# One-hot comparisons of the front read their values from 16-bit pairs stored twice, and seven comparisons of an edge chunk become one

## The chip, the cores and the metric

The kernel runs on one core of a Trainium2 chip. The metric is the device time of one execution in microseconds (us). Before the change three runs gave 1142.17, 1131.55 and 1142.92 us; the median is 1142.17 us.

## The reference

The input is a graph with N = 50,000 nodes of 128 features (`x`) and E = 25,000 edges with 16 features each. Edges are sorted by their target `dst`; `src` is random.

```python
def _edge_conv(x, src, dst, edge_attr, W, b, denom):
    msg = jnp.concatenate([x[src], edge_attr], axis=1) @ W + b
    s = jax.ops.segment_sum(msg, dst, num_segments=x.shape[0])
    return s / denom[:, None]
...
counts = jax.ops.segment_sum(jnp.ones((src.shape[0],), x.dtype), dst, num_segments=x.shape[0])
denom = jnp.maximum(counts, 1.0)
h = _edge_conv(x, src, dst, edge_attr, W0, b0, denom)
outputs = [h]
for W, b in ((W1, b1), (W2, b2), (W3, b3)):
    cat = jnp.concatenate(outputs, axis=1)
    z = _edge_conv(cat, src, dst, edge_attr, W, b, denom)
    outputs.append(z)
...
x = _layernorm(x + outputs[-1], axis=-1)
```

So four edge convolutions run one after the other, and a layer norm of `x` plus the last of them over all 50,000 rows is the output.

## The kernel before

The kernel folds the four layers' weights together, sums messages per target node ("segment"), and then follows the graph for three more hops over short lists of the nodes that matter. The change touches only the first third, the front, and one loop behind it.

**Data layout.** Edges lie as 196 columns of 128 (T = 196), one edge per partition. A unit or chunk is HALF = 7 columns, so there are UNITS = 28 of them. To sum or to look things up by a value, the kernel builds one-hot matrices on the Vector engine (DVE): it compares a row of counting numbers (`iotah`, 0 to 255 in f16) with each edge's value, and TensorE (PE) multiplies with the matrix of zeros and ones.

**The front, in three stages.** Every engine runs its own program; semaphores tie them together.

- *Word stage* (`word_ones`, lines 1051 to 1060; on PE `word_sums`, L1847). For each of the 28 chunks DVE makes three tiles: `LA` compares 128 counting numbers with `lod` (L1055, 7 x 128 elements), `OHW` compares 49 with `hid` (L1059, 7 x 49), and `OHW` is multiplied by `value` (L1060). `lod` is f16, `hid` and `value` are f32 (names of the buffers `shi` and `nlo`). PE sums them into a table of words. LA and OHW have two buffers each, and DVE may be two chunks ahead (it waits on `tab_mm`).
- *Look-up stage* (`one_hot_src`, `pick`, `gather_words`, lines 1113 to 1136; on PE `look_up`, L1866). DVE makes `OS` from rows that a DMA has spread over all partitions (L1118, loaded by SP's `load_lows`, L477), then `WORD_HOT` (L1122, 49 wide, against `his`, f32 in buffer `nhi`), the product with what PE looked up (L1131) and its sum (L1136). A serial part of short instructions on DVE follows (lines 1170 to 1215).
- *Edge stage* (the loop of lines 1456 to 1466: `edge_ones`, `list_build`, `edge_add`, `list_add`; on PE `edge_chunk`, L1836 and L1840, and `list_chunk`, L1880). Per chunk DVE makes `SA` with seven instructions, each comparing 256 numbers with one column of `rela` (L1233), `SA2` (L1254, 7 x 128, against `list_lo`, f16), two small tiles (L1256, L1258), and adds PE's sums of the chunk before to `EC` and `AC` (L1243 to L1245, L1267). Before two of them it loads a row's place into registers (L1238, L1263). Every fourth chunk it also splits edge features (L1146 to L1149).

**What runs beside it.** In all three stages the 28 units of `x` run through as well: GpSimd (POOL) gathers seven columns of 128 rows of `x` by indirect DMA (L656), ScalarE makes their one-hots, PE sums them (`x_unit`, L1819 and L1827), and ScalarE adds the sums up (L799). PE's program fixes how these interleave:

```python
for u in range(UNITS):
    x_unit(u)
    if u < LOOK_UNIT:
        for c in range(u * 5, min(u * 5 + 5, UNITS)):
            word_sums(c)
```

With LOOK_UNIT = 6 and EDGE_UNIT = 13, units 0 to 5 carry five word chunks each, units 6 to 12 four look-up chunks each, and units 13 on two edge chunks each. POOL may gather two units ahead of PE's sums. SP's queue issues the clearing and copying of `x_and_z_of_nodes` (L485, L490) between the loads of rows and edge features.

**Behind the front** come the products of all segments on PE (L1915, L1916), with the making of the lists beside them. One loop there, `needed_build` (L1419), compares with `list_lo` in the same way as L1254. Three rounds over the lists and the layer norm end the program; the change doesn't touch them.

## Time and profile before

| what | value |
|---|---|
| median of three runs | 1142.17 us (1131.55 to 1142.92) |
| the profiled execution: its span, first to last instruction | 1122.8 us |
| what lies around the span, if that execution took the median time | 19.4 us |
| DVE busy | 739.8 us, 66% |
| POOL busy | 742.0 us, 66% |
| PE busy | 513.6 us, 46% |
| ScalarE busy | 476.3 us, 42% |
| word stage, look-up stage, serial part, edge stage (from the span's start) | 36 to 112.6, 112.6 to 188, 188 to 207.7, 207.7 to 378 us |

No engine is busy all the time, so the total shares decide nothing. What a faster instruction is worth has to be read in its own stage, from what the engines wait for there.

### The profile page before, as it was taken

How to read it: one execution, taken by the hardware profiler on the slowest of the kernel's cores; microseconds unless marked ns; L12 is line 12 of the kernel's file. 1: busy time of each engine (PE TensorE's matmuls, PEld its weight loads, DVE VectorE, ACT ScalarE, POOL GpSimd, SP SyncE). 2: the span in 40 equal slices, each digit the busy share in tenths (PEclk: the TensorE clock that was granted, in tenths of full speed). 3: DMA queues.
4: the chain of work that ended last, by engine and by line, in shares of the span. 5: the costliest groups of instructions: out<-in, count | busy, mean ns of one | idle time of the engine just before them, and what ended most of it. 6: DMA issues, size and time to landing. Idle time of an engine off the chain costs nothing.

```text
span 1122.8 us, 14207 instructions
## 1 busy us (share of the span) xinstructions
PE 513.6 (46%) x3128; PEld 379.0 (34%) x3128; DVE 739.8 (66%) x2530; ACT 476.3 (42%) x1099; POOL 742.0 (66%) x669
## 2 busy tenths in 40 slices
PE   1544653578776578878775360054005664000000
PEld 0433552455555345545343250043005553000000
DVE  6788677878766776454765558566767976679100
ACT  8543343334433155556554213571547541156200
POOL 6788666377675066666676647774877773777775
PEclk9666666666566589899898665566556766555555
DMA  6895457599999046455555846995899983464111
GB/s 189 229 299 154 114 133 197 149 261 324 316 304 340 6 153 218 165 202 178 180 173 175 268 138 148 301 318 179 221 291 327 336 294 118 118 222 143 50 52 34
DMA packets 224618, 224.99 MB, mean 200 GB/s; under 512 B 19218, under 2 KB 206475, under 8 KB 224495
## 3 DMA queue, kind: packets, MB, share of 16 engines
q1 hardware_dynamic: 193551, 153.22, 44.1%
q0 software_dynamic: 26624, 44.81, 15.0%
q10 hardware_dynamic: 4320, 25.56, 5.7%
q8 instruction: 47, 0.77, 0.3%
q14 instruction: 76, 0.62, 0.2%
HBM read 117.11 MB, written 132.74 MB: 223 GB/s over the span
## 4 chain that ended last, share of the span: by engine, by line
DVE 29%; PE 24%; POOL 16%; issue 15%; DMA 7%; another core or an unknown queue 4%; ACT 2%; DVEq 2%; SPq 1%; POOLq 0%; ACTq 0%
POOL out_rows L724 5%; POOL G L685 5%; PE segp L1827 4%; POOL part_rows L698 3%; PE hp L1916 3%; DVE AC L1586 3%; DVE area L1233 3%; PE segp L1916 2%; DMA area<-x_and_z_of_nodes 2%; POOL EC L717 2%; PE lp L1840 2%; PE segp L2056 2%; PE hp L2056 2%; DVE area L1254 2%
## 5 line engine op out<-in xcount | busy, mean ns | idle before, releaser
L656 POOL DMA_INDIRECT G<-x_in,srci x196 | 229.1, 1169 | 114.3 <-issue 62.2
L668 POOL DMA_INDIRECT x_and_z_of_nodes<-area,sum_rows x144 | 146.0, 1014 | 102.3 <-ACT area L826 65.2
L854 ACT ACTIVATE area<-area,AC 128x128 f32<-128x128 f32 x299 | 117.5, 480 | 44.4 <-DVE AC L1608 37.4
L799 ACT ACTIVATE UT<-segp,UT 128x1 f32 x56 | 14.6, 261 | 207.4 <-PE segp L1827 150.6
L685 POOL DMA_INDIRECT G<-part_rows,s0r x70 | 80.1, 1144 | 27.3 <-issue 18.3
L1827 PEld LDWEIGHTS segp<-SX,G 128*128 128x128 f32 x392 | 92.9, 319 | 14.0 <-issue 5.4
L1827 PE MATMUL segp<-SX,G 128*128 128x128 f32 x392 | 94.2, 409 | 5.7 <-ACT SX L788 3.2
L2050 PE MATMUL segp<-ZERO 128*128 128x390 f16 (+1 forms) x34 | 15.3, 449 | 163.0 <-DVE EC L1628 152.5
L717 POOL DMA_INDIRECT EC<-x_and_z_of_nodes,idx x60 | 64.7, 1079 | 33.4 <-issue 17.9
L826 ACT ACTIVATE area<-hp,zero,inv 128x512 f32<-128x512 f32 x72 | 53.9, 781 | 44.4 <-PE hp L1916 15.3
L826 ACT ACTIVATE area<-segp,zero,inv 128x512 f32<-128x512 f32 x72 | 54.6, 780 | 41.2 <-PE hp L1916 20.8
L724 POOL DMA_INDIRECT out_rows<-UT,idx x60 | 59.2, 986 | 18.3 <-issue 18.3
L1916 PE MATMUL hp<-LATE,UT 128*128 128x384 f32 x144 | 64.9, 535 | 0.0
L847 ACT ACTIVATE AC<-AC,eps 128x13 f32<-128x13 f32 x30 | 9.2, 306 | 131.0 <-DVE AC L1594 95.8
L1840 PE MATMUL lp<-area 128*128 128x52 bf16 x392 | 54.7, 213 | 18.8 <-issue 8.9
L2056 PE MATMUL segp<-G,EC 128*128 128x130 f32 (+1 forms) x272 | 55.2, 368 | 17.1 <-DMA G<-part_rows,s0r 7.8
L1916 PE MATMUL segp<-LATE,UT 128*128 128x384 f32 x144 | 61.2, 508 | 0.0
L1586 DVE BATCH_NORM_STATS2 AC<-area 128x6 f32<-128x128 f32 x299 | 60.1, 278 | 0.8
L784 ACT ACTIVATE SX<-iota,rel 128x128 f32<-128x128 f32 x196 | 60.4, 395 | 0.0
L2050 PEld LDWEIGHTS segp<-ZERO 128*128 128x128 f16 x34 | 4.0, 116 | 166.6 <-DVE EC L1628 159.8
L2056 PEld LDWEIGHTS segp<-G,EC 128*128 128x128 f32 x272 | 52.2, 276 | 22.8 <-DMA G<-part_rows,s0r 9.5
L2056 PE MATMUL hp<-G,EC 128*128 128x130 f32 (+1 forms) x232 | 49.4, 380 | 16.6 <-DMA G<-part_rows,s0r 8.9
(468 smaller groups left out, 1599.5 us busy)
## 6 DMA issues: line engine op xcount, KB each, us to landing
part_rows<-area SPq DMA_DIRECT2D x36, 768.0 KB
area<-x_and_z_of_nodes SPq DMA_DIRECT2D x30, 832.0 KB
x_and_z_of_nodes<-ZERO SPq DMA_DIRECT2D x24, 1024.0 KB
x_and_z_of_nodes<-x_in SPq DMA_DIRECT2D x24, 1024.0 KB
area<-x_in SPq DMA_DIRECT2D x23, 832.0 KB
out_rows<-area ACTq DMA_DIRECT2D x23, 832.0 KB
part_rows<-ZERO SPq DMA_DIRECT2D x14, 768.0 KB
area<-src_low_rows SPq DMA_DIRECT2D x28, 224.0 KB
```

Of the source, the lines that this page charges most:

```text
L656: g.indirect_dma_start(G[:, slot, 0:D], None, x, bass.IndirectOffsetOnAxis(ap=srci[:, c:c + 1].bitcast(u32), axis=0), bounds_check=last_no ...
L668: g.indirect_dma_start(XZ2, bass.IndirectOffsetOnAxis(ap=sum_rows[:, c:c + 1], axis=0), HS3[:, b, j, 3 * D:4 * D], None, bounds_check=last ...
L685: g.indirect_dma_start(G[:, n % GS, 0:D], None, TB3, bass.IndirectOffsetOnAxis(ap=take[k][:, n:n + 1], axis=0), bounds_check=last_part, oo ...
L717: g.indirect_dma_start(LZ[:, 2 * r + w, :], None, XZ[0:N, :], bass.IndirectOffsetOnAxis(ap=node_u[:, b:b + 1], axis=0), bounds_check=last_ ...
L724: g.indirect_dma_start(out, bass.IndirectOffsetOnAxis(ap=node_u[:, b:b + 1], axis=0), own_row(b, W1), None, bounds_check=last_node, oob_is ...
L826: a.activation(HS3[:, b, j, :], PBANK[j][:, :], ACT.Identity, bias=zero1[:, 0:1], scale=inv[:, g * CG + j:g * CG + j + 1]).then_inc(s["p_a ...
L854: last = a.activation(XLS[b][:, k], XLS[b][:, k], ACT.Identity, bias=shift[:, b, r:r + 1], scale=rs[:, b, r:r + 1])
L1586: last = v.bn_stats(stat[cols, b, r, :], src_[cols, r * D:(r + 1) * D])
L1827: t.matmul(SG[q][:, bass.ds(w, P)], G[:, slot, 0:D], S[:, slot, :], start=False, stop=j == hi - 1).then_inc(s["summed"], 1)
L1840: last = t.matmul(LP[b][:, bass.ds(k + w * ES64, EP)], SA[:, b * HALF + j, w * P:(w + 1) * P], EB[:, q % 2, (c % EQ) * HALF + j, 0:EP], st ...
L1916: t.matmul(PBANK[j][:, 0:3 * D], UT[:, (g * CG + j) * P:(g * CG + j + 1) * P], M[:, :], start=False, stop=True).then_inc(s["p_mm"], 1)
L2056: last = t.matmul(bank[:, bass.ds(at_, width)], OH[:, g % OHG, j, w * P:(w + 1) * P], G[:, slot, 0:width], start=False, stop=j == 1 and w ...
```

## The change

All wide comparisons named above get a form in which every operand is 16 bits wide and its innermost step is one. Each compared value is stored twice, side by side, in f16: `low_pairs` (an own buffer in place of `lod` and `list_lo`), and `value_pairs`, `hid_pairs`, `his_pairs`, `rela_pairs`, which lie in the f32 buffers `nlo`, `shi`, `nhi` and again `nlo`. A comparison then walks over the counting numbers two at a time, and over a pair again and again, instead of over one value with step 0. The width of 49 becomes 50. The seven instructions of `edge_ones` become one over 7 x 256 elements.

```diff
+        low_pairs = sb("low_pairs", [P, CT, 2], f16)
+        in_pairs = lambda a: a[:, :].bitcast(f16).rearrange("p (t w) -> p t w", w=2)
+        value_pairs, hid_pairs, his_pairs, rela_pairs = in_pairs(nlo), in_pairs(shi), in_pairs(nhi), in_pairs(nlo)
...
-            link(v.tensor_tensor(value[:, et], bits_src[:, et], flag[:, et], ALU.mult))
+            twice = lambda a: a[:, et].unsqueeze(2).to_broadcast([P, T, 2])
+            link(v.tensor_tensor(value_pairs[:, et, :], twice(bits_src), twice(flag), ALU.mult))
-            link(v.tensor_copy(lod[:, et], ints[:, et]))
+            link(v.tensor_copy(low_pairs[:, et, :], twice(ints)))
-            link(v.tensor_copy(hid[:, et], ints[:, et]))
+            link(v.tensor_copy(hid_pairs[:, et, :], twice(ints)))
...
+            def in_twos(tiles):
+                return tiles.rearrange("p j (w t) -> p j w t", t=2)
+            def spread_pairs(pairs, c, width):
+                return pairs[:, c * HALF:(c + 1) * HALF, :].unsqueeze(2).to_broadcast([P, HALF, width // 2, 2])
+            def ones_by_pairs(tiles, pairs, c, width):
+                places = iotah[:, 0:width].rearrange("p (w t) -> p w t", t=2).unsqueeze(1).to_broadcast([P, HALF, width // 2, 2])
+                return v.tensor_tensor(in_twos(tiles), places, spread_pairs(pairs, c, width), ALU.is_equal)
...
-                v.tensor_tensor(LA[:, b, :, :], iotah[:, 0:P].unsqueeze(1).to_broadcast([P, HALF, P]),
-                                lod[:, c * HALF:(c + 1) * HALF].unsqueeze(2).to_broadcast([P, HALF, P]), ALU.is_equal)
-                link(v.tensor_tensor(OHW[:, b, :, 0:WORDS], iotah[:, 0:WORDS].unsqueeze(1).to_broadcast([P, HALF, WORDS]), spread_out(hid), ALU.is_equal))
-                v.tensor_tensor(OHW[:, b, :, 0:WORDS], OHW[:, b, :, 0:WORDS], spread_out(value), ALU.mult).then_inc(s["oh_built"], 1)
+                ones_by_pairs(LA[:, b, :, :], low_pairs, c, P)
+                link(ones_by_pairs(OHW[:, b, :, :], hid_pairs, c, WORDS + 1))
+                words = in_twos(OHW[:, b, :, :])
+                v.tensor_tensor(words, words, spread_pairs(value_pairs, c, WORDS + 1), ALU.mult).then_inc(s["oh_built"], 1)
...
-            link(v.tensor_copy(his[:, et], ints[:, et]))
+            link(v.tensor_copy(his_pairs[:, et, :], twice(ints)))
+            link(v.tensor_copy(rela_pairs[:, et, :], twice(rela)))
...
-                v.tensor_tensor(WORD_HOT[:, b, :, :], iotah[:, 0:WORDS].unsqueeze(1).to_broadcast([P, HALF, WORDS]),
-                                his[:, k].unsqueeze(2).to_broadcast([P, HALF, WORDS]), ALU.is_equal).then_inc(s["hot_words"], 1)
+                ones_by_pairs(OHW[:, b, :, :], his_pairs, c, WORDS + 1).then_inc(s["hot_words"], 1)
...
-            link(v.tensor_scalar(list_lo[:, et], wlo[:, et], -1.0, None, ALU.add))
+            link(v.tensor_scalar(low_pairs[:, et, :], twice(wlo), -1.0, None, ALU.add))
...
-                for j in range(HALF):
-                    last = v.tensor_scalar(SA[:, (c % 2) * HALF + j, :], iotah[:, :], rela[:, c * HALF + j:c * HALF + j + 1], None, ALU.is_equal)
-                last.then_inc(s["e_built"], 1)
+                ones_by_pairs(SA[:, (c % 2) * HALF:(c % 2 + 1) * HALF, :], rela_pairs, c, 2 * P).then_inc(s["e_built"], 1)
...
-                v.tensor_tensor(SA2[:, b, :, :], iotah[:, 0:P].unsqueeze(1).to_broadcast([P, HALF, P]),
-                                list_lo[:, chunk].unsqueeze(2).to_broadcast([P, HALF, P]), ALU.is_equal)
+                ones_by_pairs(SA2[:, b, :, :], low_pairs, c, P)
```

`needed_build` changes as `list_build` does (`CLO` in place of `SA2`), and its `list_lo` is made in pairs too. `pick` goes on reading 49 of the 50 columns.

No instruction changes its place among the others. On DVE, at the start of the edge stage, before the change (the buffers `SA` and `SA2` lie in `area`):

```order
L1223 CAST area<-nh 128x28
L1224 CAST area<-nl 128x28
L1225 COPY area<-flag 128x28
L1233 TENSOR_SCALAR area<-iotah,rela 128x256 x7
L1254 TENSOR_TENSOR area<-iotah,list_lo 128x896
L1256 TENSOR_TENSOR area<-iota,nodes 128x56
L1258 TENSOR_TENSOR area<-LATE,area 128x336
```

And with the change (`nlo` holds `rela_pairs`; L1064 is the comparison in `ones_by_pairs`):

```order
L1235 CAST area<-nh 128x28
L1236 CAST area<-nl 128x28
L1237 COPY area<-flag 128x28
L1064 TENSOR_TENSOR area<-iotah,nlo 128x1792
L1064 TENSOR_TENSOR area<-iotah,low_pairs 128x896
L1265 TENSOR_TENSOR area<-iota,nodes 128x56
L1267 TENSOR_TENSOR area<-LATE,area 128x336
```

The seven instructions of 256 elements are one of 1792; everything else stands where it stood. The one added instruction of the program is the copy to `rela_pairs` ahead of the look-up stage.

## Rows read from the trace of the kernel before

**Rows 1.** Stages: busy us of PE, PEld, DVE, ACT, POOL; PEclk, DMA share, GB/s.
```profile
36.00:112.60 76.60, 34.17 (x294) 29.98 (x294) 59.22 (x104) 33.61 (x101) 63.61 (x49) 0.59 0.84 239
112.60:188.00 75.40, 43.91 (x504) 38.79 (x504) 55.24 (x131) 34.48 (x105) 50.10 (x47) 0.66 0.50 130
207.70:378.00 170.30, 127.59 (x838) 93.76 (x839) 130.53 (x436) 61.59 (x189) 103.11 (x88) 0.61 0.86 261
```

**Rows 2.** Chain of waits, shares by line: word stage, look-up stage, edge stage.
```profile
by line: PE segp L1827 23.7%; DVE area L1055 20.4%; issue 15.4%; DVE area L1060 11.8%; DVE area L1059 9.8%; PE segp L1819 7.9%; PE tp L1847 7.2%; ACT SX L788 1.0%; DVE area L1107 0.5%; DVE area L1096 0.4%; PE tp L1871 0.3%; DVE area L1095 0
...
by line: issue 26.8%; PE segp L1827 18.1%; PE lp L1866 13.1%; DMA area<-src_low_rows 9.2%; DVE idx L1136 7.2%; PE segp L1819 6.0%; DVE area L1122 5.4%; DVE area L1131 4.8%; DVE area L1118 4.5%; SPq L477 1.7%; DVE area L1147 0.9%; DVE area L
...
by line: DVE area L1233 17.3%; issue 15.0%; PE lp L1840 12.1%; DVE area L1254 10.0%; PE segp L1827 8.9%; DVEq L1263 4.4%; DVEq L1238 3.5%; DVE EC L1243 3.2%; PE segp L1819 3.0%; DVE EC L1244 2.9%; DVE EC L1245 2.9%; PE lp L1836 2.7%; DVE AC
```

**Rows 3.** Groups on DVE by shape, 0 to 560 us: busy us, mean ns | idle before.
```profile
L1233 DVE TENSOR_SCALAR area<-iotah,rela 128x256 bf16<-128x256 f16 x196 | 41.4, 295 | 3.8 <-DVE AC L1267 0.6 <-issue 0.3 <-PE lp L1840 0.3
...
L1254 DVE TENSOR_TENSOR area<-iotah,list_lo 128x896 bf16<-128x896 f16 x28 | 30.3, 1081 | 0.0
...
L1258 DVE TENSOR_TENSOR area<-LATE,area 128x336 bf16<-128x336 bf16 x28 | 14.3, 509 | 1.0
...
L1118 DVE TENSOR_SCALAR area<-area,iotap 128x896 f16<-128x896 f16 x28 | 13.2, 470 | 2.3 <-DMA area<-src_low_rows 1.0 <-issue 0.7 <-DVE area L1149 0.2
...
L1146 DVE CAST area<-area 128x448 bf16<-128x448 f32 x7 | 2.7, 390 | 0.3 <-DVE area L1225 0.2
```

**Rows 4.** Timeline of DVE in the word stage, one chunk and the next: start, us.
```profile
59.49 1.08 DVE L1055 TENSOR_TENSOR area<-iotah,lod 128x896 f16<-128x896 f16 x1
60.49 0.51 DVE L1059 TENSOR_TENSOR area<-iotah,shi 128x343 f16<-128x343 f16 x1
61.04 0.52 DVE L1060 TENSOR_TENSOR area<-area,nlo 128x343 f16<-128x343 f16 x1
61.47 1.08 DVE L1055 TENSOR_TENSOR area<-iotah,lod 128x896 f16<-128x896 f16 x1
```

**Rows 5.** Timeline of PE in the word stage, from one x unit to the next.
```profile
63.55 0.58 PE L1819 MATMUL segp<-ZERO 128*128 128x512 f16 x1 [1.46 <-issue]
...
67.34 0.79 PE L1847 MATMUL tp<-area 128*128 128x49 f16 x14
70.01 0.47 PE L1847 MATMUL tp<-area 128*128 128x49 f16 x7 [1.88 <-DVE area L1060]
...
75.92 0.58 PE L1819 MATMUL segp<-ZERO 128*128 128x512 f16 x1 [1.49 <-issue]
```

**Rows 6.** Timeline of POOL in the word stage: a gather beside idle DVE, one beside L1055.
```profile
54.11 1.00 POOL L656 DMA_INDIRECT G<-x_in,srci  x1 [0.30 <-issue]
...
59.76 1.68 POOL L656 DMA_INDIRECT G<-x_in,srci  x1 [0.30 <-issue]
```

**Rows 7.** Groups on POOL by shape: word stage, then edge stage.
```profile
L656 POOL DMA_INDIRECT G<-x_in,srci x41 | 54.4, 1326 | 12.4 <-issue 12.4
...
L656 POOL DMA_INDIRECT G<-x_in,srci x88 | 103.1, 1172 | 55.3 <-issue 25.4 <-PE segp L1827 23.6 <-remote 6.3
```

**Rows 8.** Chain of waits in the look-up stage, one piece: start, us, what.
```profile
139.97 3.53 DMA area<-src_low_rows
```

**Rows 9.** Timeline of DVE in the edge stage, from one chunk to the next.
```profile
310.98 1.46 DVE L1233 TENSOR_SCALAR area<-iotah,rela 128x256 bf16<-128x256 f16 x7
312.35 1.08 DVE L1254 TENSOR_TENSOR area<-iotah,list_lo 128x896 bf16<-128x896 f16 x1
...
315.66 1.47 DVE L1233 TENSOR_SCALAR area<-iotah,rela 128x256 bf16<-128x256 f16 x7
```

**Rows 10.** Waits in the edge stage: us in total, times, longest us.
```profile
PE lp L1836 <- DVE area L1233: 9.1, 7, 3.1
```

**Rows 11.** Timeline and group on DVE: the old cast to `list_lo`; `needed_build`.
```profile
205.59 0.26 DVE L1215 TENSOR_SCALAR list_lo<-wlo 128x196 f16<-128x196 f32 x1
...
L1419 DVE TENSOR_TENSOR area<-iotah,list_lo 128x896 bf16<-128x896 f16 x10 | 11.0, 1098 | 0.0
```

More of the change, by code:

```diff
@@ L213, in gnn_kernel @@
         xoff = wlo[:, :].bitcast(i32)
-        value, hid, his, src_low = nlo, shi, nhi, idx
+        src_low = idx
+        in_pairs = lambda a: a[:, :].bitcast(f16).rearrange("p (t w) -> p t w", w=2)
+        value_pairs, hid_pairs, his_pairs, rela_pairs = in_pairs(nlo), in_pairs(shi), in_pairs(nhi), in_pairs(nlo)
         AREA = 8584
@@ L237, in gnn_kernel @@
         list_hi, list_block = nodes, inv[:, :].bitcast(i32)
-        list_lo = sb("list_lo", [P, T], f16)
         list_hi2, list_block2 = nodes, nodec[:, :].bitcast(i32)
@@ L1412, in needed_places @@
                 link(v.tensor_tensor(wlo[:, et], wlo[:, et], need[:, et], ALU.mult))
-                link(v.tensor_scalar(list_lo[:, et], wlo[:, et], -1.0, None, ALU.add))
+                link(v.tensor_scalar(low_pairs[:, et, :], twice(wlo), -1.0, None, ALU.add))
             def needed_build(c):
@@ L1418, in needed_build @@
                     e.wait_ge(s["c2_mm"], c - 1)
-                v.tensor_tensor(CLO[:, b, :, :], iotah[:, 0:P].unsqueeze(1).to_broadcast([P, HALF, P]),
-                                list_lo[:, places_of(c)].unsqueeze(2).to_broadcast([P, HALF, P]), ALU.is_equal)
+                ones_by_pairs(CLO[:, b, :, :], low_pairs, c, P)
                 one_hots(CHOT[:, b, :, :], list_hi2, c, HALF + 1).then_inc(s["c2_hot"], 1)
```

4 lines of the change are left out of this document (removed).

## The prediction, made before the changed kernel had run

> **What bounds the kernel now.** I read the table by stage first, since the change lies in the front alone. In the word stage [rows 1] DVE is busy 59.2 of 76.6 us and POOL 63.6, PE only 34.2. In the edge stage DVE is busy 130.5 of 170.3 us, PE 127.6, POOL 103.1. No engine fills a stage, so the engines must be waiting in turn, and the chain of waits is the second view [rows 2]. In the word stage it runs through the three instructions that change, L1055, L1059 and L1060: 42% of 76.6 us. In the look-up stage only 5.4% lie on L1122. In the edge stage L1233 and L1254 hold 17.3% and 10.0% of 170.3 us, with PE's L1840 (12.1%) close behind.
>
> The timelines show how a turn goes. DVE needs 61.47 - 59.49 = 1.98 us per word chunk [rows 4]. PE takes 12.37 us from one x unit to the next [rows 5]: the unit itself, two chunks that lay ready (67.34), then three more that it waits for (from 67.8 to 74.4), then 1.5 us before the next unit. DVE is only two chunks ahead, so three chunks in five are on the path. In the edge stage a chunk takes DVE 4.68 us when it never waits [rows 9], but 170.3 / 28 = 6.1 us on average.
>
> **What one instruction will take.** Two 16-bit comparisons with a step of 0, of 896 and 336 elements, take 1081 and 509 ns [rows 3]. That is 572 / 560 = 1.02 ns per element plus 166 ns. The trace has no two-input operation of the new form (16 bits, innermost step one everywhere), so its rate is bounded. The slow end is no gain, 1.02 ns. The fast end is L1118, 896 elements of one input in 470 ns: (470 - 166) / 896 = 0.34 ns. Between them lies L1146, 448 elements in 390 ns: 0.50 ns. I take 0.50, since two inputs must be fetched where L1118 fetches one, and keep both ends.
>
> The Trainium skill, "Vector Engine (DVE) Microarchitecture Reference", section 5.1, says that a two-input operation runs two elements per tick if all operands have 2 bytes, an innermost step of one and more than one element innermost, and that one element read again and again runs at one per tick. By that rule the old form is slow and the new one twice as fast. No row here shows the new half; the 1.02 ns of the old form agree.
>
> **The change, part by part.**
>
> - *Word stage.* L1055 goes from 1.08 us to 166 + 448 = 0.61 (-0.47). L1059 and L1060 each go from 0.51 to 166 + 175 = 0.34 (-0.17, with 350 instead of 343 elements). A chunk's pitch falls from 1.98 to 1.17 us. By the chain [rows 2] L1055 holds 15.6 us of the path, 15 pieces at about 1.0 us, and L1059 and L1060 7.5 and 9.0 us, 14 and 16 pieces: 15 x 0.47 + 30 x 0.17 = 12.2 us. The turn of PE [rows 5] gives the same: 3 chunks x 0.81 = 2.4 us for each of five units, and 0.8 for the last. Is something late next? POOL's gathers for a unit now end only some 7 us before PE takes it up, and POOL never waits for PE in this stage (its 12.4 us of idle are all issue, [rows 7]). A gather takes 1.00 us while DVE rests and 1.68 beside L1055 [rows 6], on average 1.33, so with 0.3 of issue a unit of seven costs POOL 11.4 us against a new turn of PE of 12.4 - 2.4 = 10.0. If DVE's holds become half as long, a gather averages perhaps 1.2 (an estimate between the 1.00 and the 1.33 of these rows), a unit 10.5 us. That nearly keeps up: I take **-12**, and -5 if the gathers stay at 1.33.
> - *Look-up stage.* L1122 loses 0.17 us; 5.4% of 75.4 us are 8 pieces on the path, so 1.4 us. But the load of the next rows takes 3.53 us [rows 8] and only two are ahead, so a faster chunk waits for it. I take **-1**.
> - *Edge stage.* The seven L1233 end 1.46 us after they start, and L1254 starts 1.37 after [rows 9]. One instruction of 1792 elements takes 166 + 896 = 1.06 us: -0.40. L1254 goes from 1.08 to 0.61: -0.47. The chain holds 29.5 us of L1233, 20 chunks, and 17.0 us of L1254, 17 chunks: 20 x 0.40 + 17 x 0.47 = 16 us at most. PE is close behind, though, with 127.6 us of work of its own; its explicit waits for L1233 add up to 9.1 us [rows 10]. The gain lies between about 5 and 16; I take **-10**.
> - *Behind the front.* L1419 runs ten times at 1.10 us [rows 11]; 10 x 0.48 = 4.8 us, beside PE's products. I take **-1**.
> - *Added.* The five stores in pairs and the one copy more handle 392 elements instead of 196. The cast to `list_lo` takes 0.26 us [rows 11], so each costs at most that much more. Those ahead of the word and look-up stages lie where DVE would be ahead of PE, the one at L1215 is on a serial path. Without the cover all would cost 1.5 us; I take **+0.5**.
>
> The sum is -12 - 1 - 10 - 1 + 0.5 = -23.5 us. The profiled execution's span is 1122.8 us; the new one would be 1099. The time around the span (19.4 us if that execution was the median one) doesn't change, so against the median of 1142.17 I predict **1118 us**. Runs of before lie 1% apart, so 1% is about what a measurement can tell from no change.
>
> Transfers must not be late either. The copies of `x_and_z_of_nodes` fill DMA in the edge stage (share 0.86 on average, [rows 1]). They aren't on its chain of waits, and POOL's scatters that need them come after 378 us, so I count nothing.
>
> **The rivals.**
>
> *The next in line takes over (chance 0.25).* POOL stays at 1.33 us per gather and PE's own work sets the edge stage. Then -5 in the word stage, -6 in the edge stage, nothing elsewhere: about 1131 us. For it: POOL is the busiest engine of the word stage, and PE and DVE are nearly equal in the edge stage. Against it: POOL's slow gathers stand beside DVE's long instructions, which get shorter.
>
> *The pairs run no faster (0.07), the case on the slower side.* If two inputs stay at 1.02 ns in this form too, L1055 and L1254 gain nothing, and one instruction of 1792 elements takes 166 + 1828 = 1.99 us in place of 1.46, since the seven of 256 ran at 1.46 / 1792 = 0.8 ns and lost that rate with their scalar. On 20 chunks of the path that is +11 us, with the casts about +12: 1154 us. Where does it turn? At a rate of 0.72 ns, (1460 - 166) / 1792, the new instruction takes as long as the old seven, and the other pieces on the path still gain; with them the sum reaches zero at about 0.88 ns per element. For it: no row shows the form. Against it: 16-bit operands of step one with one input do run fast.
>
> *More than the sum (0.08).* If the comparisons come near L1118's rate, or shorter holds bring the gathers to 1.0 us, each stage gives more: the instruction of 1792 would take 0.78 us (0.28 more on 20 chunks, 5.6 us), L1055 and L1254 0.14 more on 32 pieces (4.6 us). -34 us, 1108.
>
> A longer hold of POOL is the other side of the edge stage: one DVE instruction of 1.06 us where seven short ones left gaps. The trace agrees that a gather gets longer beside L1055 (1.68 against 1.00 us). In the edge stage gathers average 1.17 us and POOL waits for PE 23.6 us [rows 7], so 88 gathers could each grow by 0.2 us and stay hidden; hence no term.
>
> **How the numbers follow.** The forecast has a chance of 0.60 (its own range 1112 to 1125), the rivals 0.25, 0.07 and 0.08. Faster by over 1% means below 1130.7: all of the forecast and of the larger gain, over half of the first rival: 0.83. Within 1%: the rest of that rival, 0.10. Slower: 0.07. The range of 8 in 10 takes in the first rival and half of the larger gain: 1105 to 1134.
>
> **What would show it.** In the profile after, the comparison of 896 elements takes about 0.61 us, that of 1792 about 1.06, those of 350 about 0.34; the word stage lasts 64 to 65 us and the edge stage 160; gathers of the word stage fall from 1.33 us on average towards 1.2; PE's waits for the edge comparisons shrink; behind the front all stages last as long as before. The prediction is wrong if the 896 take more than 0.8 us, or if POOL's gathers or PE's issue fill the time that DVE frees.

## The result, and the profile after the change

The change gained nothing. In 20 runs each, one beside the other, the kernel before took 1137.62 us (median) and the changed one 1142.36 us; the ratio is 1.006, with a 95% interval of 1.0035 to 1.0085. Here and below the ratios leave out runs in the slower state, over 1.5% above the fastest of their kernel (one of `after_few` took 2280.08 us), so they aren't exactly the quotients of the medians. I had predicted 1118 us and a range that ended at 1134.

The profiled execution of the changed kernel has a span of 1148.2 us, that of before 1122.8 us. Such a pair exaggerates the difference, so I compare parts. Let the **front** end where DVE adds the last list chunk to `AC` (L1267 before, L1276 after). It ended at 375.9 us before and at 385.7 us after. What lies behind took 746.8 us before. In the 16 further profiles below that leave the transfers in place it was 742 to 750 us, with the change and without it, and only here 762.5 us. So some 15 us of the difference belong to this one execution, and the change itself acts in the front alone. That is what I read below. A stage's time in one profile is uncertain too: the four kernels below that have the word stage, the gathers and the transfers as they were (before, edge_only, edge_seven, old_word) end it at 110.0 to 112.6 us.

The instructions did what was forecast. Groups on DVE of the changed kernel, 0 to 600 us (busy us, mean ns | idle before), against [rows 3]:

```profile
L1064 DVE TENSOR_TENSOR area<-iotah,nlo 128x1792 bf16<-128x1792 f16 x28 | 30.6, 1094 | 3.7
...
L1064 DVE TENSOR_TENSOR area<-iotah,low_pairs 128x896 bf16<-128x896 f16 x38 | 23.6, 621 | 0.0
...
L1064 DVE TENSOR_TENSOR area<-iotah,low_pairs 128x896 f16<-128x896 f16 x28 | 18.4, 656 | 41.0 <-PE tp L1855 22.9 <-remote 18.1
...
L1073 DVE TENSOR_TENSOR area<-area,nlo 128x350 f16<-128x350 f16 x28 | 10.9, 388 | 1.0
...
L1064 DVE TENSOR_TENSOR area<-iotah,shi 128x350 f16<-128x350 f16 x28 | 9.3, 334 | 0.0
```

1094, 621 and 334 ns stand where 1.06, 0.61 and 0.34 us were forecast. (1094 - 621) / 896 is 0.53 ns per element; I had taken 0.50, and the old form ran at 1.02. By the Trainium skill's rule that the prediction quoted ("Vector Engine (DVE) Microarchitecture Reference", section 5.1) the new form is twice as fast, and the trace agrees. But look at the idle time in the third line: DVE stood still for 41.0 us ahead of the word comparison. The stages, as in [rows 1] (busy us of PE, PEld, DVE, ACT, POOL; PEclk, DMA share, GB/s):

```profile
36.00:118.90 82.90, 33.65 (x293) 29.49 (x294) 37.85 (x103) 33.85 (x101) 53.05 (x48) 0.58 0.79 222
118.90:201.20 82.30, 46.65 (x504) 40.85 (x504) 50.60 (x133) 34.62 (x105) 50.92 (x49) 0.65 0.46 125
220.60:387.80 167.20, 127.11 (x840) 93.65 (x840) 107.63 (x267) 61.97 (x190) 97.20 (x89) 0.59 0.87 265
```

In the word stage DVE's work fell from 59.2 to 37.9 us and POOL's from 63.6 to 53.1, yet the stage grew from 76.6 to 82.9 us. The look-up stage with the serial part grew from 94.7 to 101.3 us (both from the start of unit 6 to the first payload copy of the edge stage), and the edge stage shrank from 170.3 to 167.2. In the word stage no engine's work grew by more than 0.3 us. The chain of waits of the word stage, by line, names the new holder, against [rows 2]:

```profile
by line: another core or an unknown queue 23.2%; PE segp L1835 18.3%; issue 16.8%; DVE area L1064 16.3%; DVE area L1073 7.8%; PE tp L1855 6.1%; PE segp L1827 5.4%; ACT SX L789 0.9%; DVE area L1109 0.3%; DVE area L1098 0.3%; DVE area L1090 0
```

"Another core or an unknown queue" (in the timelines: "remote") isn't among the lines of this chain before. There is only one core, so the label means that the profile found no row that ended just before the wait did. The timelines of three engines at one place show what it stands for. DVE of the changed kernel in the word stage (start, us):

```profile
48.23 0.35 DVE L1073 TENSOR_TENSOR area<-area,nlo 128x350 f16<-128x350 f16 x1
58.35 0.63 DVE L1064 TENSOR_TENSOR area<-iotah,low_pairs 128x896 f16<-128x896 f16 x1 [9.77 <-remote]
...
62.16 0.63 DVE L1064 TENSOR_TENSOR area<-iotah,low_pairs 128x896 f16<-128x896 f16 x1 [2.56 <-remote]
...
65.87 0.63 DVE L1064 TENSOR_TENSOR area<-iotah,low_pairs 128x896 f16<-128x896 f16 x1 [2.46 <-remote]
```

PE at the same place:

```profile
50.84 1.48 PE L1835 MATMUL segp<-SX,G 128*128 128x128 f32 x6
52.12 0.64 PE L1855 MATMUL tp<-area 128*128 128x49 f16 x14
59.66 0.47 PE L1855 MATMUL tp<-area 128*128 128x49 f16 x7 [6.91 <-DVE area L1073]
```

And POOL, the last gathers of a series of 14:

```profile
61.46 1.00 POOL L657 DMA_INDIRECT G<-x_in,srci  x1 [0.30 <-issue]
62.76 1.15 POOL L657 DMA_INDIRECT G<-x_in,srci  x1 [0.30 <-issue]
73.94 1.15 POOL L657 DMA_INDIRECT G<-x_in,srci  x1 [10.03 <-PE segp L1835]
```

PE's 14 products end at 52.76 us (as modelled), and two increments of `tab_mm`, the semaphore that DVE waits for, go with them. DVE needs the first of them and starts at 58.35, more than 5 us later; the second releases it at 62.16. The trace records the increments themselves at 58.33 and 62.14 us. The next product, over at 60.13, is told at 65.85. POOL's gathers end at 63.9, and from 65.93 us on nothing is behind (the product that ends at 67.66 is told at 67.67). So a word from PE travels for microseconds while POOL issues gathers.

I counted this over the whole front. An increment of PE is **late** here if the trace records it more than 0.25 us after the end of the last instruction of PE that makes it and has ended by then. (Where several increments are held up together this counts from the last product, so it gives too small delays rather than too large ones.) In the profile of before, of those made during a series of gathers or within 1 us behind one, 133 of 228 are late, by up to 7.7 us; of the 55 made at other times, none. In the other direction the words are prompt: no increment of DVE in the front of before is recorded more than 0.03 us behind its row, and 34 of PE's 38 starts that DVE releases follow within 0.06 us. The other four, all products of the look-up, start 0.84 to 3.02 us behind DVE's row.

In the edge stage PE's own issue stutters as well. PE of the changed kernel while a series of gathers runs (to 252.87 us), and behind it:

```profile
248.39 0.22 PE L1848 MATMUL lp<-area 128*128 128x52 bf16 x1 [1.87 <-issue]
249.13 0.22 PE L1848 MATMUL lp<-area 128*128 128x52 bf16 x1 [0.52 <-issue]
250.75 0.22 PE L1848 MATMUL lp<-area 128*128 128x52 bf16 x1 [1.40 <-issue]
251.40 0.22 PE L1848 MATMUL lp<-area 128*128 128x52 bf16 x1 [0.43 <-issue]
253.48 0.20 PE L1848 MATMUL lp<-area 128*128 128x52 bf16 x1 [1.85 <-issue]
254.18 0.20 PE L1848 MATMUL lp<-area 128*128 128x52 bf16 x1 [0.49 <-issue]
255.13 0.84 PE L1848 MATMUL lp<-area 128*128 128x52 bf16 x4 [0.74 <-issue]
255.87 0.44 PE L1888 MATMUL hp<-area 128*128 128x48 bf16 x7
```

Single products with up to 1.9 us of "issue" between them, and then seven in 0.44 us. DVE's add of that chunk (L1253) waited 12.27 us for them.

The Trainium skill, "Perfetto Trace Analysis", section "Summary: the profiler window per engine type", says that TensorE's row ends at an estimate, and that the time until a semaphore has arrived is hidden from the row. The trace agrees: no row above covers the time between the product that ends at 52.76 and the waiter that starts at 58.35. The page doesn't say how long that time may be.

### The profile page after: what moved, and what is told of

The parts are those of the page before. It is cut to its first block, busy times and chain, and to the rows that moved or that the text cites. A ratio compares the mean times of both kernels' runs of the same rounds, so it can differ in the third digit from the quotient of the medians.

```text
span 1148.2 us, 14017 instructions
## 1 busy us (share of the span) xinstructions
PE 507.1 (44%) x3105; PEld 374.1 (33%) x3128; DVE 683.6 (60%) x2363; ACT 478.0 (42%) x1099; POOL 727.5 (63%) x669
## 4 chain that ended last, share of the span: by engine, by line
DVE 28%; PE 24%; issue 15%; POOL 12%; another core or an unknown queue 9%; DMA 7%; ACT 2%; DVEq 1%; SPq 0%; POOLq 0%; ACTq 0%
POOL out_rows L725 5%; PE segp L1835 4%; DVE AC L1594 4%; POOL part_rows L699 4%; DVE area L1064 3%; PE hp L1924 3%; PE segp L1924 3%; PE lp L1848 3%; DMA area<-x_and_z_of_nodes 3%; DVE area L1609 2%; POOL EC L718 2%; DVE UT L1650 1%; PE segp L1827 1%; PE hp L2064 1%
## 5 line engine op out<-in xcount | busy, mean ns | idle before, releaser
L657 POOL DMA_INDIRECT G<-x_in,srci x196 | 210.2, 1073 | 144.9 <-PE segp L1835 66.4
L1848 PE MATMUL lp<-area 128*128 128x52 bf16 x392 | 54.7, 214 | 27.4 <-issue 17.7
L1064 DVE TENSOR_TENSOR area<-iotah,low_pairs 128x896 bf16<-128x896 f16 (+1 forms) x66 | 42.0, 636 | 41.0 <-PE tp L1855 22.9
L848 ACT ACTIVATE AC<-AC,eps 128x13 f32<-128x13 f32 x30 | 9.2, 307 | 137.1 <-DVE AC L1602 108.1
L2064 PE MATMUL segp<-G,EC 128*128 128x130 f32 (+1 forms) x272 | 52.7, 356 | 29.3 <-DMA G<-part_rows,previ 13.1
L699 POOL DMA_INDIRECT part_rows<-UT,nlo x24 | 44.8, 1865 | 20.7 <-DVE UT L1705 13.7
```

The source lines that it names most:

```text
L657: g.indirect_dma_start(G[:, slot, 0:D], None, x, bass.IndirectOffsetOnAxis(ap=srci[:, c:c + 1].bitcast(u32), axis=0), bounds_check=last_no ...
L699: g.indirect_dma_start(TB3, bass.IndirectOffsetOnAxis(ap=l2_at[k - 1][:, b:b + 1], axis=0), own_row(b, w), None, bounds_check=last_part, o ...
L1848: last = t.matmul(LP[b][:, bass.ds(k + w * ES64, EP)], SA[:, b * HALF + j, w * P:(w + 1) * P], EB[:, q % 2, (c % EQ) * HALF + j, 0:EP], st ...
L2064: last = t.matmul(bank[:, bass.ds(at_, width)], OH[:, g % OHG, j, w * P:(w + 1) * P], G[:, slot, 0:width], start=False, stop=j == 1 and w ...
```

## The experiments

All ratios are to the kernel before, run beside each kernel on the same chip, with 95% intervals; it took 1122 to 1127 us there, 1137.62 beside the changed kernel. The table collects what the sections use. "Unit 6" is the start of the seventh x unit on PE, the end of the word stage; "late" is the share of PE's increments between 36 us and the end of the front that are late, and the last column sums the delays of all of them. Each row but the ratio is from one profile.

| kernel | ratio | unit 6 | front ends | late | delays, us |
|---|---|---|---|---|---|
| before | | 112.6 | 375.9 | 48% | 259 |
| changed | 1.006 (1.0035 to 1.0085) | 118.9 | 385.7 | 52% | 346 |
| before_late | 1.119 (1.113 to 1.126) | 106.6 | 382.0 | 37% | 164 |
| after_late | 1.119 (1.113 to 1.126) | 111.0 | 374.1 | 53% | 321 |
| word_only | 1.0046 (1.0006 to 1.0085) | 116.8 | 379.7 | 49% | 261 |
| edge_only | 0.9946 (0.9916 to 0.9977) | 110.0 | 369.9 | 54% | 312 |
| edge_seven | 1.0011 (0.9982 to 1.0040) | 111.0 | 382.0 | 48% | 281 |
| old_word | 1.0007 (0.9975 to 1.0039) | 112.4 | 373.7 | 47% | 283 |
| word_pad | 1.0035 (1.0005 to 1.0066) | 113.7 | 377.8 | 49% | 284 |
| word_ring | 1.0003 (0.9968 to 1.0037) | 109.9 | 378.5 | 54% | 399 |
| after_ring | 1.0037 (1.0004 to 1.0070) | 111.0 | 378.4 | 54% | 400 |
| before_few | 0.9751 (0.9706 to 0.9796) | 111.8 | 355.8 | 1% | 6 |
| after_few | 0.9486 (0.9443 to 0.9529) | 99.4 | 321.1 | 0% | 5 |
| before_pause | 1.0050 (1.0022 to 1.0078) | 112.7 | 387.4 | 25% | 118 |
| after_pause | 0.9963 (0.9921 to 1.0006) | 111.7 | 372.9 | 32% | 146 |
| after_pause_again | 0.9930 (0.9895 to 0.9964) | 110.7 | 369.2 | 32% | 146 |
| after_two | 0.9952 (0.9923 to 0.9980) | 109.1 | 366.4 | 22% | 48 |
| before_each | 0.9930 (0.9899 to 0.9961) | 111.0 | 371.5 | 26% | 83 |
| after_each | 0.9814 (0.9756 to 0.9872) | 108.1 | 356.6 | 45% | 188 |
| after_tick | 1.0089 (1.0053 to 1.0124) | 118.8 | 385.3 | 52% | 355 |

### Are the transfers the pace? before_late and after_late

```diff
-            clear_sums(range(0, Z_AT[0]))
...
             for q in range(2, NQ):
                 load_features(q)
-                copy_x(range((q - 2) * XPIECES // (NQ - 2), (q - 1) * XPIECES // (NQ - 2)))
+            clear_sums(range(0, XPIECES))
+            copy_x(range(0, XPIECES))
```

> The kernel before, with all 25 clearing and 25 copying transfers of x_and_z_of_nodes issued after the last load of edge features, so that none runs beside the front. Same work, other order. Theory A (transfers set the pace of the front): before them the front had DMA shares of 0.76 and 0.87 in word and edge stage; without them the x units come faster, and unit 27, which started at 374.8 us, starts before 355 us. Theory B (PE's hand-offs to DVE or the engines' own work set it): unit 27 starts within 5 us of 374.8. The whole is slower in either case, since some 50 MB that moved at 300 GB/s then stand by themselves: 1230 to 1310 us. The run serves as the partner of after_late.

> The changed kernel with the same transfers put behind the front. Theory A: what DVE saves now reaches the end of the front: unit 27 starts 12 to 22 us ahead of before_late's, and the whole takes 10 to 22 us less than before_late. Theory B (late hand-offs, or gathers of POOL, eat the gain without any help from the transfers): within 5 us of before_late, both at unit 27 and in the whole.

Measured: unit 27 started at 382.1 us in before_late, where theory A wanted less than 355 and B 370 to 380, and at 374.4 in after_late. The transfers aren't the pace of the front: A falls. But they aren't without effect, as B has it. The word stage ended 6.0 and 7.9 us sooner without them (106.6 and 111.0 us), and after_late's unit 27 came 7.7 us before before_late's, between what A (12 to 22) and B (less than 5) had asked. What before_late lost behind the word stage stays open. The two whole times are the same (1252.68 and 1253.65 us), but that tells little, since the moved transfers form the end of this stretch in both and can hide what the front gives. Late words from PE are as frequent in after_late (53%), with a DMA share of 0.15 to 0.33 from 46 to 90 us, as in the changed kernel with 0.97 to 1.07, so DMA traffic alone isn't what makes them late (in before_late 37% were, against 48% in before).

### Which stage loses? word_only, edge_only, edge_seven, old_word

Each undoes part of the change. word_only keeps only the word stage's pairs:

```diff
-                ones_by_pairs(OHW[:, b, :, :], his_pairs, c, WORDS + 1).then_inc(s["hot_words"], 1)
+                v.tensor_tensor(WORD_HOT[:, b, :, :], iotah[:, 0:WORDS].unsqueeze(1).to_broadcast([P, HALF, WORDS]),
+                                his[:, k].unsqueeze(2).to_broadcast([P, HALF, WORDS]), ALU.is_equal).then_inc(s["hot_words"], 1)
...
-                ones_by_pairs(SA[:, (c % 2) * HALF:(c % 2 + 1) * HALF, :], rela_pairs, c, 2 * P).then_inc(s["e_built"], 1)
+                for j in range(HALF):
+                    last = v.tensor_scalar(SA[:, (c % 2) * HALF + j, :], iotah[:, :], rela[:, c * HALF + j:c * HALF + j + 1], None, ALU.is_equal)
+                last.then_inc(s["e_built"], 1)
```

> Only the word stage in pairs; look-up, edge stage and the loop behind the front as before. The word comparison of 896 elements takes 0.62 us. By my prediction, had it held, 12 us less than before (1.1%). Theory A: the transfers fill the word stage up to 90 us and the edge stage from 183 us; the word stage gives little and the edge stage takes back what is left: within 4 us of before. Theory C (a faster word stage disturbs what comes later: DVE's operations collide with POOL's gathers or its waits for PE get longer): slower than before by 3 to 8 us, so that the whole loss of the change is here.

edge_only has both edge comparisons (and the loop behind the front) in pairs, the word and look-up stages as before:

> Only the edge stage (and the loop behind the front) in pairs, the word and look-up stages as before. My prediction gave 10 us less. Theory A (the copies of x_and_z_of_nodes fill DMA from 183 us on, share 0.87, and SP's loads of edge features stand in the same queue behind them): within 4 us of before. Theory D (one operation of 1.09 us holds up POOL's issue of gathers where seven short ones left gaps): slower by 3 to 8 us, gathers of the edge stage over 1.25 us on average instead of 1.17.

edge_seven is edge_only with the seven short comparisons put back:

> edge_only with the seven short comparisons kept, so that only the comparison of 896 elements in the edge stage (and the loop behind the front) is in pairs. edge_only was 6 us faster than before. If the two edits give what they save on the path, this one gives about half: -3 us. If one operation of 1792 elements is what helps: within 2 us of before. If the one long operation hurts and the shorter list comparison helps: 6 us or more faster than before.

old_word is the changed kernel with the old word stage:

> The changed kernel with the word stage as before (old form, old values) and the look-up stage, the edge stage and the loop behind the front in pairs. edge_only, which lacks the look-up stage's pairs, was 6 us faster than before. If the word stage alone is what costs: 4 to 9 us faster than before. If the look-up comparison costs too: within 2 us of before.

Measured: the word stage's pairs cost 0.46%, about 5 us (theory C's size). The profiles agree: with the pairs the word stage ended at 116.8 us (word_only) and 118.9 (changed), without them at 110.0 to 112.6. The edge stage's give 0.54%, 6 us, so theory D falls, and A's "within 4 us" too. The one wide operation makes the gain: without it (edge_seven) nothing is left, where I had expected 3 us. old_word, with the look-up's pairs besides, is at 1.0007 where 4 to 9 us less were expected if the word stage alone costs. So the look-up's comparison, 0.17 us shorter, seems to cost 0.6% against edge_only (the two intervals leave 0.0 to 1.2%, and the two kernels ran on different chips). In the profiles the stretch from unit 6 to the first payload copy lasts 99.6 us in old_word, 101.3 in the changed kernel and 100.7 in after_ring, against 94.6 to 95.9 in before, edge_only, word_only and word_pad, which keep the old look-up; but edge_seven and word_ring, which keep it too, have 99.1 and 99.6. So the word stage loses by a faster DVE, and the look-up stage probably does, by about 4 us; that isn't shown clear of the noise.

### The pace or the form? word_pad

```diff
+                link(v.tensor_tensor(LA[:, b, :, 0:88], iotah[:, 0:88].unsqueeze(1).to_broadcast([P, HALF, 88]),
+                                     low_pairs[:, c * HALF:(c + 1) * HALF, 0:1].to_broadcast([P, HALF, 88]), ALU.is_equal))
                 ones_by_pairs(LA[:, b, :, :], low_pairs, c, P)
```

> word_only with one superfluous comparison more per word chunk, in the old form over 7 x 88 elements (about 0.79 us by 166 ns + 1.02 ns per element), so that DVE's pitch per chunk is again about 1.96 us, with the pairs kept. Theory P (the pace: DVE two chunks ahead no longer covers a late word from PE; with DVE slow it does): unit 2 starts at 62 to 65 us again instead of 69, and the whole is within 2 us of before. Theory F (the form of the operations: 16-bit pairs disturb another engine whatever the pace): unit 2 still starts near 69 us, and the whole stays 4 us or more above before.

Measured: unit 2 started at 65.7 us, between the 63.5 of before and the 69.0 of word_only, and unit 6 at 113.7 instead of 116.8. A DVE slowed down with work of no use brought the stage three of its four lost us back, with the pairs in place. So in the word stage the pace matters more than the form, as far as one profile each can tell: 3.1 us is little more than the 2.6 by which equal word stages differ. The whole (1.0035 against 1.0046) doesn't decide it.

### More cover? word_ring and after_ring

```diff
-                b = c % 2
-                if c >= 2:
-                    e.wait_ge(s["tab_mm"], c - 1)
-                ones_by_pairs(LA[:, b, :, :], low_pairs, c, P)
+                if c >= 4:
+                    e.wait_ge(s["tab_mm"], c - 3)
+                ones_by_pairs(LAR[c % 4], low_pairs, c, P)
```

`LAR` and `OHR` take their third and fourth buffers from `SA` and `ECS`, which are free in this stage.

> word_only with four buffers for LA and OHW instead of two, so that DVE may be four chunks ahead of PE. Theory L (PE's increments reach DVE 2 to 6 us after PE's last product of the chunk, which two buffers can't bridge): with four, a late one is bridged; unit 2 starts before 62 us, the word stage is 6 to 12 us shorter than in word_only, the whole 4 to 12 us faster than before. Theory Q (PE itself is behind its modelled ends, its own rate bounds the stage): no gain, unit 2 again near 69 us and the whole 3 to 6 us above before.

> The changed kernel with the same four buffers in the word stage. Theory L: the edge stage's gain, which edge_only showed (-6 us), and the word stage's add up: 10 to 18 us faster than before. Theory Q: within 3 us of the changed kernel (+5 us).

Measured: unit 2 started at 51.8 us, 17 us ahead of word_only, as L said. Then it was given back: unit 3 at 69.7, unit 6 at 109.9. The whole is at 1.0003 against word_only's 1.0046, not the 4 to 12 us below before that L named; after_ring, at 1.0037, is where Q put it. DVE of word_ring where it was lost:

```profile
58.60 0.62 DVE L1071 TENSOR_TENSOR area<-iotah,low_pairs 128x896 f16<-128x896 f16 x1 [5.82 <-PE tp L1866]
...
64.57 0.62 DVE L1071 TENSOR_TENSOR area<-iotah,low_pairs 128x896 f16<-128x896 f16 x1 [4.72 <-PE tp L1866]
```

Seven increments of unit 2's sums, whose products end between 53.7 and 58.3 us, are recorded from 65.94 to 66.21 us, 0.045 us apart, although a sum takes 0.43 us: those products had long been done, and the words came in one burst. POOL's series ended at 64.0. Both theories were half right: buffers bridge a late word, but here the hold-up lasted to the end of POOL's series, and four buffers don't reach that far.

### Without the gathers: before_few and after_few

```diff
-                for j in range(HALF):
+                for j in range(HALF if u < 2 else 1):
...
-                            e.wait_ge(gat[u % 2 * 4 + j // 2], (32 if j < HALF - 1 else 16) * (u // 2 + 1))
+                            e.wait_ge(gat[u % 2 * 4 + j // 2], (32 if j < HALF - 1 else 16) + (16 * (u // 2) if j == 0 else 0))
```

> The kernel before with only one gather of x rows per unit from unit 2 on instead of seven; the other six columns use rows that were gathered for units 0 and 1, so the sums of x are not the reference's, while all the work of PE, DVE and ScalarE stays. Theory G (POOL's gathers hold up PE's increments: in the profile of before 133 of the 228 increments of PE that fall in or within 1 us behind a series of gathers are over 0.25 us late, and none of the 55 outside): without the series at most a tenth of PE's increments in the front are over 0.25 us late, and unit 27 starts 15 us or more ahead of 374.8 us. Rival R (PE's own work is behind its modelled ends): as many are late as before, up to 5 us, and unit 27 moves by less than 10 us.

> The changed kernel with the same gathers left out. Theory G: PE's increments come in time here too, and what DVE saves reaches the end of the front: unit 27 starts 15 to 30 us ahead of before_few's, and the whole takes 12 to 30 us less than before_few. Rival R, or a bound by PE's own work: less than 5 us between the two.

Both kernels leave out six of seven gathers from unit 2 on, and so sum rows of `x` that aren't the right ones.

Measured: late words fell from 48% and 52% to 1% and 0%, with PE's program untouched, and unit 27 of before_few started at 354.7 us, 20 earlier. Between the two kernels there are now 0.9751 - 0.9486 = 0.0265 of 1126.2 us, 30 us: the gain that I had predicted (23.5), and more (the medians, 1103.17 and 1070.46 us, lie 33 us apart). Unit 27 of after_few came 33 us before before_few's. Windows of before_few, word stage and edge stage:

```profile
36.00:111.80 75.80, 33.03 (x294) 28.99 (x294) 58.41 (x104) 34.45 (x102) 18.51 (x13) 0.62 0.77 212
190.00:356.00 166.00, 122.03 (x830) 90.83 (x831) 130.57 (x438) 63.48 (x193) 12.48 (x12) 0.64 0.81 243
```

And of after_few:

```profile
36.00:99.40 63.40, 32.66 (x294) 28.76 (x294) 37.26 (x103) 34.31 (x102) 15.32 (x13) 0.67 0.92 253
180.00:321.00 141.00, 112.21 (x824) 85.39 (x824) 105.58 (x266) 61.67 (x188) 13.82 (x12) 0.69 0.92 278
```

The word stage is 12.4 us shorter; the prediction said 12. The edge stage, from its first payload copy to the front's end, fell by 22.9 us (163.6 to 140.7), where I had said 10 and 16 at most. Two things can be behind the excess, and no run parts them. With PE in time, more of DVE's chunks may have been on the path than the chain of before showed. And in these windows the granted clock was 0.69 in after_few against 0.64, and PE was busy for 112.2 us instead of 122.0 with nearly the same products, so up to 10 us of PE's work may have gone with the clock. The word stage is free of this: there PE's work is 32.7 against 33.0 us. PE's turn at the place of [rows 5] is the one that I had drawn, two chunks at once and three at 1.17 us each:

```profile
52.19 0.79 PE L1855 MATMUL tp<-area 128*128 128x49 f16 x14
54.03 0.35 PE L1855 MATMUL tp<-area 128*128 128x49 f16 x7 [1.05 <-issue]
55.19 0.35 PE L1855 MATMUL tp<-area 128*128 128x49 f16 x7 [0.81 <-DVE area L1073]
56.36 0.35 PE L1855 MATMUL tp<-area 128*128 128x49 f16 x7 [0.81 <-DVE area L1073]
```

Theory G holds, R falls. This pair changes several things at once, though: POOL's work and the gathers' transfers leave the path too. The next runs keep all gathers.

### Gaps between the gathers: after_pause, before_pause, after_two

```diff
                     slot = c % BODY
+                    if j == 3:
+                        for _ in range(5):
+                            plink(g.memset(rest[:, :], 0.0))
```

`plink` makes POOL wait for each memset; `rest` is a tile of its own. before_pause has the same edit in the kernel before, and after_two asks for `j in (2, 5)`.

> The changed kernel with a pause in each series of gathers: five short POOL memsets of 128 x 128 f32, each waited for, ahead of the fourth gather of a unit (some 1 to 1.5 us per unit). Theory G: PE's increments that were held up come through in the pause, so the longest delay falls from 11 us to about half a series (5 us); the time moves by -10 to +15 us, since POOL's series gets longer by the pause, and is no test by itself. Rival R: the pause changes nothing in when they come.

> The same kernel as after_pause, in more rounds beside the three others: 0.996 of before, interval within 0.4% of it.

> The kernel before with the same pause (five short memsets ahead of the fourth gather of a unit). Theory G: in the word stage DVE's long operations already stretch and part the gathers, so that few increments of PE are late there, and PE's late ones are in the look-up and edge stages; the pause lengthens POOL's series by 1.5 us per unit and gives back less than with the fast DVE: within 4 us of before. Rival H (the pause helps whatever DVE does): 4 us or more faster than before, as much as it gave the changed kernel.

> The changed kernel with two pauses in each series, ahead of the third and the sixth gather (2 x 1.5 us per unit). Theory G: the delays get shorter still (sum under 146 us in the front), but POOL's series of 9.2 us becomes 12.3, longer than the 11.3 us that a unit takes, so POOL's own work bounds the edge stage: 0 to 12 us slower than with one pause.

Measured: giving POOL more to do made the changed kernel faster, from 1.006 of before to 0.9963 and 0.9930 in two sets. The sum of the delays fell from 346 to 146 us, the longest from 11.2 to 6.5. In before the same pause cost 0.5%, 6 us, a little more than the 4 that G allowed. That is the crossed result that G wanted and H excluded: the pause helps with the fast DVE and costs with the slow one, although it cut the delays there as well (259 to 118 us). Two pauses cut the delays to 48 us, and the time is the same as with one (0.9952), presumably since POOL's longer series takes back what the words give.

### Small gaps: after_each, before_each, after_tick

after_each puts one memset, waited for, ahead of each gather but the first of a unit. before_each does it in the kernel before. after_tick has no memset, only an increment of POOL's own semaphore and the wait for it:

```diff
+                    if j:
+                        plink.n += 1
+                        e.sem_inc(s["pool_chain"], 1)
+                        e.wait_ge(s["pool_chain"], plink.base + plink.n)
```

> The changed kernel with one short memset, waited for, ahead of each gather but the first of a unit (6 x 0.25 us per unit, as long in all as the one pause). Theory G with gaps of any length: increments come through at each gap, sum of delays below 146 us, time at or below that with one pause. If a gap must last about 1 us: the delays stay as in the changed kernel (over 250 us in all) and the time is 3 to 10 us above before.

> The kernel before with one short memset, waited for, ahead of each gather but the first of a unit, as in after_each (0.981 of before). Theory G (gaps let PE's increments through, and the changed kernel gains most because its fast DVE left the gathers closest together and waits for PE most): before_each lies between, 0 to 10 us faster than before, so that the change itself is worth 10 us or more between before_each and after_each. Rival S (the gaps are worth the same with or without the change, 20 to 25 us): 0.975 to 0.985 of before.

> The changed kernel with no memset but an increment of POOL's own semaphore and a wait for it ahead of each gather but the first. If what counts is that POOL's queue runs empty between two gathers, even for 0.1 us: as after_each, 0.977 to 0.987 of before. If it is the time that the memset adds to the gap (the next gather starts 0.49 us after the last instead of 0.30): little, 1.000 to 1.007, as the changed kernel.

POOL of after_each in the word stage:

```profile
50.94 0.22 POOL L660 MEMSET rest<- 128x128 f32 x1
51.43 1.00 POOL L661 DMA_INDIRECT G<-x_in,srci  x1 [0.27 <-POOL rest L660]
52.43 0.22 POOL L660 MEMSET rest<- 128x128 f32 x1
52.92 1.00 POOL L661 DMA_INDIRECT G<-x_in,srci  x1 [0.27 <-issue]
```

Measured: with a gather every 1.49 instead of every 1.30 us the changed kernel takes 0.9814 of before, 1106.33 against 1126.31 us; it is the best version found. Without the change the same gaps give 0.9930. So with gaps the change is worth about 1.2%, some 13 us, and without them it costs 0.6%. after_tick, at 1.0089, gained nothing, and its profile tells why it couldn't:

```profile
48.32 0.99 POOL L661 DMA_INDIRECT G<-x_in,srci  x1 [0.30 <-issue]
49.62 0.99 POOL L661 DMA_INDIRECT G<-x_in,srci  x1 [0.30 <-issue]
```

Its gathers stand 1.30 us apart, as without the tick: the increment and the wait disappear in the 0.30 us that were there, so this run made no gap. It shows that one more wait in POOL's program does nothing, but not whether a gap without an operation in it would help. One figure missed: the delays of after_each sum to 188 us, not below 146, and 45% are late. So the count of late words doesn't order the times; I take it that what counts is whether the word that somebody waits for is late, but no count here shows that. The windows of after_each (word and edge stage):

```profile
36.00:108.10 72.10, 33.45 (x294) 29.29 (x294) 38.99 (x103) 33.61 (x101) 58.73 (x84) 0.62 0.89 254
201.10:358.70 157.60, 124.51 (x838) 92.56 (x839) 107.57 (x268) 61.54 (x189) 115.71 (x165) 0.64 0.93 283
```

72.1 and 157.6 us, where the prediction had 64 to 65 and 160.

## Why the prediction was wrong

**Durations of the new form: right.** 0.62 to 0.66, 1.09 and 0.33 us, for 0.61, 1.06 and 0.34. Only the product (L1073, 388 ns) stayed above its 0.34. Two of the inputs were loose: the 0.50 ns per element came from a cast of one input (L1146), and L1258, which I called a comparison, is a product. "The pairs run no faster", my one rival on the slower side, named the wrong cause.

**The word stage, -12 us: this step failed.** It was worked out from the chain and from PE's turn as rows show it, and both take it that DVE may go on when PE's row ends; the time for PE's word to arrive was put at nothing. In before that was nearly so: of the 65 increments of PE in the word stage 8 were late, and DVE's two chunks of lead at 1.98 us each covered them. With chunks of 1.17 us the lead is used up sooner, DVE waits, and what it waits for is under POOL's series: 11 of 61 increments were late in the word stage of the changed kernel, and all delays of the stage sum to 25 us instead of 7. The stage grew by 6.3 us in the profile of the changed kernel; the pairs of this stage alone cost 5 us in time. With the gathers out, and the late words with them, the same edit gave the 12 us (12.4, before_few and after_few), so the working was right but for this one assumption.

**The next in line.** My sign of being wrong named POOL's gathers or PE's issue as what might fill DVE's time; in the word stage it was the own work of neither, but PE's words during the gathers; in the edge stage PE's issue, slowed during the gathers, had a part. I asked whether POOL's gathers would be fast enough, and noted that they take 1.00 us beside an idle DVE and 1.68 beside L1055. They did get faster, 1.06 us on average in the word stage instead of 1.33. I booked that as a help, and in the rival "more than the sum" even as a larger gain. I now read it as part of the harm: the gathers then stand 1.30 us apart without a break, and it feeds itself. DVE waits for PE's word, so it disturbs no gather, so the series runs undisturbed, so the word stays away until it ends. In before, L1055 kept stretching gathers to 1.68 us ([rows 6]), and no word of the stage was over 1.9 us late, though its 41 gathers form one series. This loop is my reading of word_pad, after_pause and before_pause together; no run shows it alone.

**The look-up stage, -1:** its part is about +6 by the times, uncertain by as much (edge_only against old_word), and about +4 by the profiles. The stage was already full of late words before: bursts at 138.6 and 149.9 us, each about 1 us behind a series of gathers.

**The edge stage, -10:** -6 us (edge_only), between the 5 and the 16 given, and 22.9 once the gathers are out (after_few), part of which may be the clock. In the profiles the stage, from the payload copy to the front's end, went from 168.6 to 165.5 us in the changed kernel and to 155.9 with gaps (after_each), so the gathers without gaps held it down too.

**Behind the front, -1, and the stores, +0.5:** nothing seen; the part behind the front is 742 to 750 us with and without the change, a scatter that would hide both.

**The time around the span** was 19.4 us in the prediction. It is 1.7 us (a run of 1141.02 us has a span of 1139.3); the profiled execution of before was a short one (about 1124.5 us, below all 20 runs of the result), not the median. This moved no term of the sum.

## What to carry to other kernels

- Before you book the gain of a faster producer, measure how late the word of its consumer comes, not when the consumer's row ends: take waits labelled as remote or unknown on a single core, compare the waiter's start with the end of the row that releases it, and see what another engine issues just then.
- An engine that gets faster can take away a cover that nobody had planned. Here a slow DVE hid late words and, as I read it, also kept them short by stretching the gathers.
- Long series of indirect gathers issued back to back can cost more than their own time; one memset of 0.22 us between two of them took the changed kernel from 1.006 to 0.981 of before, and the kernel before to 0.993.

## What was not expected of the hardware

While POOL issues indirect gathers 1.30 us apart, PE's increments reach their waiters up to 11.9 us late (after_ring), sometimes singly, often all together about 1 us behind the last gather, 0.045 us apart; increments of DVE are recorded within 0.03 us in the same stretches. PE's own issue stutters too, with gaps up to 1.9 us between single products. From 200 to 380 us PE's idle time put down to "issue" ahead of the edge products (L1840, in the changed kernel L1848) is 8.9 us in before, 17.4 in the changed kernel, and 3.6 and 2.9 in before_few and after_few. Leaving out six of seven gathers thus removes the late words and nearly all of the stutter, and a gap of 0.49 us in place of 0.30 between gathers brings the changed kernel to 20 us below before.

Why this is so stays open. The burst of word_ring suggests that products were done and only the words missing; the single products of the edge stage suggest that PE's issue is held as well. Through what, no run tells. Nor do the runs tell how much the recording of spans has to do with it, since each time here was taken with its span and clock recorded. The Trainium skill, "NOTIFIC — the notification-queue block", section 7.1, says that the internal pipeline of the block that writes notification records always holds back its producers rather than lose a record inside the block; no run here shows whether that is at work.
